# An LSTM layer with residual on one core: all gates of a step in one PSUM bank, the chain between steps by halves of the features

## The reference

```python
xW = jnp.einsum('ntd,dk->tnk', x, Wx) + b
def step(carry, xw_t):
    prev_h, prev_c = carry
    a = xw_t + prev_h @ Wh
    i = jax.nn.sigmoid(a[:, :Hdim]); f = jax.nn.sigmoid(a[:, Hdim:2 * Hdim])
    o = jax.nn.sigmoid(a[:, 2 * Hdim:3 * Hdim]); g = jnp.tanh(a[:, 3 * Hdim:])
    next_c = f * prev_c + i * g
    next_h = o * jnp.tanh(next_c)
    return ((next_h, next_c), next_h)
_, hs = jax.lax.scan(step, (h0, c0), xW)
return x + jnp.transpose(hs, (1, 0, 2))
```

## Time and profile before

| | |
|---|---|
| median of 3 runs | 2559.55 us |
| the profiled execution | 2560.61 us |
| its span, first to last instruction | 2558.8 us |
| TensorE matmuls busy | 2534.1 us, 99% |
| VectorE busy | 1947.6 us, 76% |
| ScalarE busy | 1023.5 us, 40% |
| granted TensorE clock | 1.00 of full speed |
| DMA | 30 GB/s on average |

### The profile page before, as it was taken

The page is one execution under the profiler, slowest core; times in us unless marked ns, Lnnn a source line. Parts: engine busy times, 40 slices in busy tenths (PEclk is TensorE's granted clock), DMA queues, the critical chain, the costliest instruction groups (busy, mean ns, idle before and its releaser), DMA issues.

```text
span 2558.8 us, 199267 instructions
## 1 busy us (share of the span) xinstructions
PE 2534.1 (99%) x90967; PEld 2458.9 (96%) x90967; DVE 1947.6 (76%) x6293; ACT 1023.5 (40%) x3233; POOL 0.2 (0%) x4
## 2 busy tenths in 40 slices
PE   7999999999999999999999999999999999999998
PEld 3599999999999999999999999999999999999998
DVE  7777777777777777777777777777777777777776
ACT  5433433333334333333333334434433343334333
POOL 0000000000000000000000000000000000000000
PEclk9999999999999999999999999999999999999999
DMA  4101101011010010110110101101101011011000
GB/s 171 36 17 33 25 25 33 16 33 33 16 33 25 25 33 16 33 33 16 33 25 24 33 16 33 33 16 33 28 21 33 19 30 33 16 33 31 18 16 18
DMA packets 141430, 76.30 MB, mean 30 GB/s; under 512 B 8536, under 2 KB 140248, under 8 KB 140504
## 3 DMA queue, kind: packets, MB, share of 16 engines
q1 hardware_dynamic: 140692, 75.53, 11.2%
q10 hardware_dynamic: 708, 0.33, 0.0%
HBM read 42.27 MB, written 33.55 MB: 30 GB/s over the span
## 4 chain that ended last, share of the span: by engine, by line
PE 98%; DMA 1%; DVE 0%; SPq 0%; issue 0%; ACT 0%; DVEq 0%
PE if_odd L267 25%; PE if_even L274 13%; PE if_odd L274 13%; PE og_even L274 13%; PE og_odd L274 13%; PE s1t_sum L267 6%; PE if_even L267 6%; PE og_even L267 6%; DMA w_raw<-in_L_cond_Wh_dram 1%; PE if_even L303 1%; PE if_even L288 1%; PE plain_even L303 1%; PE plain_even L288 1%; SPq L237 0%; ACT hw_hi L513 0%
## 5 line engine op out<-in xcount | busy, mean ns | idle before, releaser
L633 DVE TENSOR_TENSOR i_g<-i_f,g_gate 128x128 f32<-128x128 f32 x512 | 149.7, 292 | 416.3 <-ACT g_gate L477 416.3
L267 PE MATMUL if_odd<-xw_hi,xT_lo 128*32 128x256 f16 x7936 | 401.9, 273 | 0.2 <-issue 0.2
L267 PE MATMUL if_odd<-xw_lo,xT_hi 128*32 128x256 f16 x7936 | 401.9, 273 | 0.1
L267 PE MATMUL if_odd<-xw_hi,xT_hi 128*32 128x256 f16 x7936 | 401.8, 273 | 0.0
L485 ACT ACTIVATE tanh_c<-c_state 128x128 f32<-128x128 f32 x512 | 158.6, 310 | 195.4 <-DVE c_state L635 195.4
L267 PEld LDWEIGHTS if_odd<-xw_lo,xT_hi 128*32 128x32 f16 x7936 | 227.6, 97 | 0.3 <-issue 0.3
L267 PEld LDWEIGHTS if_odd<-xw_hi,xT_hi 128*32 128x32 f16 x7936 | 227.5, 97 | 0.5
L267 PEld LDWEIGHTS if_odd<-xw_hi,xT_lo 128*32 128x32 f16 x7936 | 227.4, 97 | 0.5 <-issue 0.4
L440 ACT ACTIVATE if_even<-if_odd 128x256 f32<-128x256 f32 x248 | 91.3, 368 | 253.4 <-PE if_odd L267 253.4
L473 ACT ACTIVATE i_f<-if_odd 128x256 f32<-128x256 f32 x248 | 95.9, 387 | 225.0 <-PE if_odd L274 225.0
L631 DVE TENSOR_TENSOR f_c<-i_f,c_state 128x128 f32<-128x128 f32 x512 | 149.2, 291 | 34.4 <-ACT i_f L473 12.9
(11 more groups left out here) (115 smaller groups left out, 5973.4 us busy)
## 6 DMA issues: line engine op xcount, KB each, us to landing
x_ring<-in_x_dram SPq DMA_DIRECT2D x252, 128.0 KB, 2.8
out_dram<-x_ring SPq DMA_DIRECT2D x252, 128.0 KB
w_raw<-in_L_cond_Wh_dram SPq DMA_DIRECT2D x4, 1024.0 KB, 17.0
w_raw<-in_L_cond_Wx_dram SPq DMA_DIRECT2D x3, 1024.0 KB, 9.9
w_raw<-in_L_cond_Wx_dram SPq DMA_DIRECT2D x2, 512.0 KB, 5.2
x_ring<-in_x_dram SPq DMA_DIRECT2D x6, 64.0 KB, 19.0
out_dram<-x_ring SPq DMA_DIRECT2D x5, 64.0 KB
out_dram<-x_ring SPq DMA_DIRECT2D x4, 48.0 KB
```

The costliest lines, as they stand in the source:

```text
L267: mm = nc.tensor.matmul(bank[j * N:(j + 1) * N, 0:HALF], x_part[:, pair, n, k * N:(k + 1) * N], w_part[:, n, k, j, :], start=start and g = ...
L633: nc.vector.tensor_tensor(i_g[:, :], i_f[:, 0:P], g_gate[:, :], ALU.mult).then_inc(i_g_ready, 1)
```

## The change

All gates of a step lie in one bank: i and f in its columns IF (0 to 255), o and g in OG (256 to 511), even[p] and odd[p]. The recurrence uses groups of 512 columns, and has one semaphore, gates_ready, at its end. It takes hT_hi first, k = 0 and 1 as soon as these 64 columns of hT_hi are there (hT_hi_ready[0]), then k = 2 and 3, then all of hT_lo. From the gates to hT_hi, everything but the sigmoid of o is done by halves: half 0 is what k = 0 and 1 need, in each tile the columns 0 and 1 of every four, half 1 the columns 2 and 3 (half_of). The bias difference is no longer added by VectorE: ScalarE seeds s1t1_sum with it ahead of the product (seed_s1t1, odd steps, last in its queue) and copies the sum out (take_s1t1, even steps, after tanh). fill_og_odd moves behind the transposes of h, S2 behind the half of A12, and the four combines spread over steps 1, 2, 2 and 3 of every four instead of 1, 1, 2 and 2. The first 16 steps keep their order, with a bank of their own for odd steps. The core of the diff:

```diff
-        if_even = [psum(f"if_even{p}", [P, G], F32) for p in range(2)]
-        if_odd = [psum(f"if_odd{p}", [P, G], F32) for p in range(2)]
-        og_even = psum("og_even", [P, G], F32)
-        og_odd = psum("og_odd", [P, G], F32)
+        even = [psum(f"even{p}", [P, G], F32) for p in range(2)]
+        odd = [psum(f"odd{p}", [P, G], F32) for p in range(2)]
         s1t1_sum = psum("s1t1_sum", [P, G], F32)
         plain_even = psum("plain_even", [P, G], F32)
-        plain_odd = if_even[1]
+        plain_odd = psum("plain_odd", [P, G], F32)
+        IF, OG = slice(0, HALF), slice(HALF, G)
...
+        def half_of(a, two):
+            return a.rearrange("p (e k) -> p e k", k=J)[:, :, 2 * two:2 * two + 2]
...
-            def recur_add(bank, half, hT, w, k):
+            def recur_add(bank, hT, w, k):
                 for j in range(J):
-                    mm = nc.tensor.matmul(bank[j * N:(j + 1) * N, 0:HALF], hT[:, k * N:(k + 1) * N],
-                                          w[:, k, j, half * HALF:(half + 1) * HALF],
+                    mm = nc.tensor.matmul(bank[j * N:(j + 1) * N, :], hT[:, k * N:(k + 1) * N], w[:, k, j, :],
                                           start=False, stop=False, skip_group_check=True)
...
             def recur(t, s):
-                banks = banks_of(s)
-                pe.wait_ge(hT_hi_ready, now)
-                for half in range(2):
-                    for w in (hw_hi, hw_lo):
-                        for k in range(J):
-                            recur_add(banks[half], half, hT_hi, w, k)
-                    if not half:
-                        pe.wait_ge(hT_lo_ready, now)
-                    for k in range(J):
-                        mm = recur_add(banks[half], half, hT_lo, hw_hi, k)
-                    mm.then_inc((if_gates_ready, og_gates_ready)[half], 1)
+                bank = (odd if s % 2 else even)[s // 2 % 2]
+                for two, count in enumerate((now, since)):
+                    pe.wait_ge(hT_hi_ready[two], count)
+                    for k in range(2 * two, 2 * two + 2):
+                        for w in (hw_hi, hw_lo):
+                            recur_add(bank, hT_hi, w, k)
+                pe.wait_ge(hT_lo_ready, now)
+                for k in range(J):
+                    mm = recur_add(bank, hT_lo, hw_hi, k)
+                mm.then_inc(gates_ready, 1)
...
-                    pe.wait_ge(s1t1_ready, q - PAIR0)
-                product(s1t1_sum, P_S1, p, start=True).then_inc(s1_done, 1)
+                pe.wait_ge(s1t1_seeded, q + (1 - PAIR0))
+                pe.wait_ge(late_ready, q + (1 - PAIR0))
+                product(s1t1_sum, P_S1, p).then_inc(s1_done, 1)
                 pe.wait_ge(if_even_ready, q + (1 - PAIR0))
-                product(if_odd[p], P_S2, p).then_inc(s2_done, 1)
-                pe.wait_ge(late_ready, q + (1 - PAIR0))
-                product(if_even[p], P_A12, p, last=3)
+                product(even[p], P_A12, p, last=3)
+                product(odd[p], P_S2, p).then_inc(s2_done, 1)
...
+            def seed_s1t1(q):
+                nc.scalar.activation(s1t1_sum[:, IF], bias_diff[:, :], ACT.Copy).then_inc(s1t1_seeded, 1)
...
+            def take_s1t1(q):
+                act.wait_ge(s1_done, q + (1 - PAIR0))
+                if not isinstance(q, int) or q > PAIR0:
+                    act.wait_ge(og_odd_ready, q - PAIR0)
+                nc.scalar.activation(s1t1[:, :], s1t1_sum[:, IF], ACT.Copy).then_inc(s1t1_ready, 1)
...
+                    for two in range(2):
+                        i_f_half, bank_half = [a.rearrange("p (g e k) -> p g e k", g=2, k=J)[:, :, :, 2 * two:2 * two + 2]
+                                               for a in (i_f[:, :], bank[:, IF])]
+                        nc.scalar.activation(i_f_half, bank_half, ACT.Sigmoid,
+                                             scale=UNSCALE).then_inc(if_ready[two], 1)
+                        nc.scalar.activation(half_of(g_gate[:, :], two), half_of(bank[:, 3 * P:4 * P], two), ACT.Tanh,
+                                             scale=UNSCALE).then_inc(g_ready[two], 1)
...
+                    forget(0, now)
+                    remember(0, now)
+                    forget(1, since)
+                    take_in(0, now)
+                    remember(1, since)
+                    take_in(1, since)
...
+                    for two, count in enumerate((now, since)):
+                        if two == 0 or plain_steps <= 0:
+                            dve.wait_ge(tanh_c_ready[two], count)
+                        if left:
+                            nc.vector.tensor_tensor(half_of(h_hi[:, :], two), half_of(o_gate[:, :], two),
+                                                    half_of(tanh_c[:, :], two), ALU.mult).then_inc(h_hi_ready[two], 1)
+                            transpose_h(h_hi_ready[two], h_hi, hT_hi, hT_hi_ready[two], (t + 2, t + (2 - PLAIN))[two],
+                                        2 * two, 2)
```

More of the change, by code:

```diff
@@ L259, in _, with product @@
         def _(pe):
-            def product(bank, n, pair, first=0, last=6, start=False):
+            def product(bank, n, pair, cols=IF, first=0, last=6):
                 for g in range(first, last):
@@ L368, in open_pair @@
                 pe.wait_ge(early_ready, q + (1 - PAIR0))
-                product(if_odd[p], P_A11, p).then_inc(a11_done, 1)
+                product(odd[p], P_A11, p).then_inc(a11_done, 1)
             def middle(q, p):
@@ L419, in _ @@
             pe.wait_ge(zeros_ready, 1)
-            for bank in (plain_even, *if_even, *if_odd, og_even, og_odd):
+            for bank in (plain_even, plain_odd, *even, *odd):
                 mm = nc.tensor.matmul(bank[:, :], zeros[:, 0:P], zeros[:, :], start=True, stop=True)
@@ L480, in step @@
+                nc.scalar.activation(o_gate[:, :], bank[:, 2 * P:3 * P], ACT.Sigmoid,
                                      scale=UNSCALE).then_inc(o_ready, 1)
                 if s % 2 and left >= 4 and plain_steps <= 3:
-                    act.wait_ge(if_ready, t + 1)
+                    if plain_steps <= 0:
+                        act.wait_ge(if_ready[1], since)
                     seed(r % 2)
-                act.wait_ge(c_ready, t + 1)
-                nc.scalar.activation(tanh_c[:, :], c_state[:, :], ACT.Tanh).then_inc(tanh_c_ready, 1)
+                if plain_steps > 0:
+                    act.wait_ge(c_ready[0], now)
+                    nc.scalar.activation(tanh_c[:, :], c_state[:, :], ACT.Tanh).then_inc(tanh_c_ready[0], 1)
+                else:
+                    for two, count in enumerate((now, since)):
+                        act.wait_ge(c_ready[two], count)
+                        nc.scalar.activation(half_of(tanh_c[:, :], two), half_of(c_state[:, :], two),
+                                             ACT.Tanh).then_inc(tanh_c_ready[two], 1)
@@ L556, in _, with transpose_h @@
         def _(dve):
-            def transpose_h(ready, part, to, done, count):
+            def transpose_h(ready, part, to, done, count, first=0, tiles=J):
                 dve.wait_ge(ready, count)
-                nc.vector.transpose(to[:, :].rearrange("p (k e) -> p k e", k=J),
-                                    part[:, :].rearrange("p (e k) -> p k e", k=J)).then_inc(done, 1)
+                k = slice(first, first + tiles)
+                nc.vector.transpose(to[:, :].rearrange("p (k e) -> p k e", k=J)[:, k, :],
+                                    part[:, :].rearrange("p (e k) -> p k e", k=J)[:, k, :]).then_inc(done, 1)
             def transpose_x(group, g, odd):
@@ L625, in step, with take_in @@
+            def take_in(two, count):
+                dve.wait_ge(i_g_ready[two], count)
+                nc.vector.tensor_tensor(half_of(c_state[:, :], two), half_of(i_g[:, :], two), half_of(f_c[:, :], two),
+                                        ALU.add).then_inc(c_ready[two], 1)
             def step(t, s, left, c):
                 q, r, group = c * (CHUNK // 2) + s // 2, s // 2, c * 2 + s // GROUP
-                now = t + 1 if isinstance(t, int) else dve.snap(t + 1)
+                now, since = t + 1, t + (1 - PLAIN)
+                if not isinstance(t, int):
+                    now, since = dve.snap(now), dve.snap(since)
@@ new lines, in step @@
+                if plain_steps > 1:
+                    dve.wait_ge(tanh_c_ready[0], now)
+                    nc.vector.tensor_tensor(h_hi[:, :], o_gate[:, :], tanh_c[:, :], ALU.mult).then_inc(h_hi_ready[0], 1)
+                    transpose_h(h_hi_ready[0], h_hi, hT_hi, hT_hi_ready[0], t + 2)
+                else:
+                    for two, count in enumerate((now, since)):
+                        if two == 0 or plain_steps <= 0:
[5 more added lines that the diff above has]
+                                        2 * two, 2)
@@ L667, in step @@
                     if s % GROUP == 1 and whole:
-                        combine_first(ahead, g)
```

(6 more changed lines are left out.)

161 lines of the change are left out of this document (72 added, 89 removed).

## The result

The changed kernel took 2540.86 us (median of 4 executions, 2540.53 to 2541.1) against 2559.56 for the kernel before on the same chip: ratio 0.9927, 95% interval 0.9914 to 0.9939. That is 18.7 us less where 14.9 were forecast, and 0.6 us under the low end of the range. The profiled execution took 2540.86 us too.

The account below looks back on a forecast made before the run. TensorE, busy 99% with nearly gapless matmuls, was taken to bound the kernel. The profiled 2560.61 us less 14.9 for wider products gave 2545.7; that execution stood 1.06 above the median, so 2544.7 us, range 2541.5 to 2565.

Parts of the forecast that it names:

- 512 columns: Loop recurrence in 12 groups of 512 columns instead of 24 of 256: 30 ns a step, 14.9 us saved.
- The gates wait for everything: One semaphore frees all four gates, so the sigmoid joins the chain; undivided, each step would be 0.26 us late.
- The halves: Chain by 64-column halves: recurrence's weight load 1.96 us after the first sigmoid (A), 2.06 due, so hidden at no cost.
- VectorE's queue: VectorE loses one add, gains five halved instructions (0.9 us busy time): still hidden, busy share 76% to about 90%.
- ScalarE's new jobs: ScalarE's seed and copy of S1 T1 end before they are wanted; TensorE starts no product early or late.
- Start and end: Step 14 gains about 0.3 us, path after the last recurrence about 0.4 longer: together nothing, 0 +/- 0.5 us.
- rival 3: A larger gain, which would need gaps in TensorE before the change; it was given no chance.
- Rivals 1 and 2: First: halves at half speed, 2778 us, chance 0.18; second: loads late by the saving, 2555 to 2564 us, chance 0.06.

Follow-up runs that it names:

- r256: The changed kernel with only the loop's recurrence back in 256-column products: 2560.77 us, ratio 1.0005 to the kernel before.
- whole: The changed kernel with the chain undivided, each operation as one instruction and one wait for hT_hi: 2667.25 us.
- add_late: The changed kernel with S1 T1 added by VectorE again, behind the second transpose of h_hi, and ScalarE's seed and copy gone: 2541.2 us.
- singles: The changed kernel with halves of every second element (columns 0 and 2 of every four, then 1 and 3) instead of adjacent pairs: 2541.01 us.
- last_whole: The changed kernel with the last step's chain undivided, as before had it: 2541.0 us.
- w_outer: The changed kernel with the recurrence's old order, all four row blocks by hw_hi, then all by hw_lo: 2541.15 us.

## Why the prediction was right and where it was wrong

- **512 columns: right.** 30 ns a step forecast, 30.0 measured; 12 groups take 2.59 us, 215.8 ns each, as in the first stage. The Trainium skill's rule on warm matmuls (TensorE: Matmul & The Clock Gate, "Wait — 56ns, not 53.3ns?") gave the same sum, and r256 agrees with it.
- **The gates wait for everything: right.** 0.26 us a step forecast for the undivided chain, 0.255 in the run whole.
- **The halves: right in the sum, off in the parts.** VectorE's took 207 to 227 ns (240 forecast), ScalarE's 239 for the tanh of g and 270 for tanh_c (225 forecast), the transposes 246 (250). The operand was ready at A + 1.85, not 1.96; the second half's transpose ends at A + 2.20, the one of lo at 3.05 (3.25 forecast). Fixed costs per instruction, as the Trainium skill has them (VectorE: DVE Perf Modes, "The TRN2 errata — SBUF-src ops pay a fixed extra latency per instruction"), fit VectorE: its 224 ns is c_state's to the digit.
- **VectorE's queue: right that it does not bind** (0.76 us idle before f*c above), wrong in its share: 78%, not about 90%. The halves do add 2 x (227 + 218 + 224 + 207 + 246) - (291 + 293 + 293 + 292 + 315) = 760 ns of durations a step; but they start 140 ns apart while one lasts 220, and busy time counts an overlap once.
- **ScalarE's new jobs: right** that they wait on nobody's path; add_late shows that they were not needed either.
- **Start and end, "together nothing: 0 +/- 0.5": this step failed.** The tail cost 0.43 us (0.4 forecast). From the recurrence of step 14 to that of step 15 it takes 6.82 us where it took 7.16, 0.34 less (0.3 forecast), and the next one 0.15 less; the other 0.3 of the 0.80 lies ahead of step 14, where the profiled executions of the changed kernel and of four near variants (singles, add_late, last_whole, w_outer) stand up to 0.7 us apart, so it is no gain that can be put down to the change. What the forecast left out is the 4.58 us at the entry and the exit of TensorE's loop, where before waited for its instructions. They stood in the trace: the wait of 1.0 us in the earlier trace rows was read as one stray gap "with no producer behind it", the view that it is from also named issue waits of 0.7 and 0.2 us, and rival 3 was dismissed since "rows 3 have none". I had read the waits after 125 us, not the lengths of the first and last steps, 5.3 to 6.1 us where 4.91 is steady. A smaller part is the chain at the end: the step ahead of the last recurrence became 0.18 us shorter (4.85 to 4.67), where 0.03 was forecast. An issue wait is time of the bounding engine like any other, and a change that removes a quarter of its instructions acts on it. The range took its low end from the rounding of one saving alone and left no room for this.
- **Rivals 1 and 2** did not come: neither half-speed halves nor a wait for hT_hi in the loop. Rival 3, a larger gain, needed gaps in TensorE; they were there, and it is what came.

## What to carry to other kernels

When one engine is busy for 99%, look also at the last 1%: list its step lengths at the entry and exit of each loop, and count its instructions as a supply with a rate (here 256 of TensorE's, matmuls and loads, per 3.7 to 4.0 us in straight code), not only as work. Here a loop body that stayed in place was cheap and a larger one was not (1440 against 2112 instructions): check the bytes of the instruction queue before unrolling. And splitting a chain into halves pays where the consumer can begin on the first; other jobs in the same queue must then stand behind the halves.

## What the runs showed of the hardware that was not expected

- A loop body of 2112 or 2880 matmuls and loads was fetched anew each iteration (10 and 13 packets of 16 KB) and cost 6.8 and 11.0 us an iteration; bodies of 1056 and 1440 were fetched once.
- Straight-line code of 180 matmuls and as many loads a step made gaps of up to 0.36 us every 3.7 to 4.0 us, one for each 16 KB packet of instructions (128 matmuls and their loads); with 132 a step it made none in sixteen steps.
- The first passage through a loop body and the code behind the loop had such gaps too, up to 1.39 us long (r256, behind its loop), each ended 1.2 to 1.6 us after a packet had landed (before, r256).
- VectorE's 64-column operations took the same time on every second element as on pairs, within 9 ns.
